# A four-layer post-norm stack on one core: projections and first row maxima in one stage, the first attention's last pair served by VectorE

## The chip, the cores and the metric

The kernel runs on one core of one Trainium2 chip. The metric is the device time of one execution in microseconds. TensorE (PE in the rows) has a weight load of its own (PEld); DVE is VectorE, ACT ScalarE, POOL GpSimd, SP SyncE, which here only issues DMAs.

## The reference

Four layers follow each other on x of 2 x 2048 x 256 float32, each with a residual and a layer norm: softmax attention with a decay, a quantized gated FFN, a linear attention, a mixture of experts. The change lies in the first alone:

```python
N_HEAD = 16                                    # hd = 16
q = (x @ Wq.T + bq).reshape(B, T, H, hd)       # k and v likewise
scores = jnp.einsum('bqhd,bkhd->bhqk', q, k) * scale
decay = jnp.exp(-alpha * jnp.abs(idx[:, None] - idx[None, :]))
attn = jax.nn.softmax(scores * decay, axis=-1)
out = jnp.einsum('bhqk,bkhd->bqhd', attn, v).reshape(B, T, D)
x = _layernorm(x + (out @ Wo.T + bo), axis=-1)
```

## The kernel before

The first attention works on 16 **pairs** of heads (8 for each of the two batches) and is built in four blocks, each closed by a barrier of all engines.

**Clearing.** In `open_sems` GpSimd clears and steps every semaphore, one after the other, while the other engines wait.

**`stage_tables`.** GpSimd writes distances (`toep`, `grow`, `c4`) and the unit matrix `ident`, ScalarE takes exponentials, VectorE splits the inverse decays into three bfloat16 parts, and SyncE stores them in DRAM as `w6`. `toep` holds the decay of every distance, so that any 128x512 piece of the decay matrix is a slice of it.

**`stage_project`.** A hardware loop over 8 chunks of 512 tokens. For each chunk and each half `jt` of the 256 columns TensorE multiplies out q and k into `ps_qk`; ScalarE adds the bias (L245, L248) into `full`; GpSimd makes the copies LEFT and RIGHT of q, scaled by `grow` (L269). Each of the four variants RAW, KEY, LEFT, RIGHT is then split into three bfloat16 parts whose sum is the float32 value: ScalarE casts the high part (L256), VectorE subtracts it (`rest`, L287), casts the middle part (L291) and subtracts again for the low part (L294). SyncE writes `part` to DRAM (`scr`, four DMAs of 384 KB a half; L201). The values v go to `vsb` (L300) and in one DMA a batch to `vscr` (L210). VectorE first clears all of `vsb`.

**`stage_attention`, first block.** GpSimd clears rows of both `p2` buffers (L497), SyncE loads `w6` into them.

**`stage_attention`, second block.** SyncE loads pair 0: `p1` (12 DMAs, L539), `p1` of pair 1 (12), `p2` (12 of L549 and 6 of L539), the values. Before a pair's scores are exponentiated, the maximum of every row is needed: 128 **tiles** a pair, each one matmul of 96x128 by 96x512 (L635) into one of three banks of `ps_r`, and one VectorE operation that multiplies by a slice of `toep` and takes the maximum (L702, with a short read of the accumulator behind it). `fold` reduces the 128 results, `turn` transposes them, and VectorE splits them (L714 to L722); SyncE stores them and loads them back as extra rows of `p2` (L575) and, broadcast, as `mb` (L577). Body `first` of `walk` does 128 tiles of pair 0 and 26 of pair 1 (`SKEW`) with nothing beside them; bodies `lead`, `mid`, `late` interleave the 64 score units of a pair with the tiles of the next; body `last` has units alone.

A **unit** is 512 queries of both heads by 128 keys: two matmuls into one of two halves of `ps_s` (L657), the exponential, and eight value matmuls a unit (L673). 48 of a pair's 64 units are exponentiated by ScalarE right from PSUM (L791). The 16 that straddle the diagonal take another way: ScalarE copies the scores to `tb` (L781), GpSimd multiplies by `toep` (L749) and adds `mb` (L752), ScalarE exponentiates (L788). The order of the units is written out in `SCORE_ORDER` and `EXP_ORDER`; `tb` has four places. After 16 units ScalarE evacuates the sums (L768), TensorE transposes them (L680), VectorE divides (L730, L732).

## Time and profile before

| | us |
|---|---|
| median of 3 runs (3662.7 to 3696.17) | 3683.9 |
| the profiled execution: its time | 3656.15 |
| its span, first to last instruction | 3654.5 |
| first tile of the row maxima | 274.7 |
| first score of pair 0 | 377.7 |
| last evacuation of pair 15 | 1887.8 |

Over the span TensorE is shown busy for 85%, VectorE for 69%, ScalarE for 48% and GpSimd for 40%. Such shares are means over stages that differ: until 377.7 us there is projection and row maxima, until 1888 us the attention of 16 pairs, behind it the other three layers. A matmul's length in the rows is partly modelled, so that TensorE's share reads high.

### The profile page before, as it was taken

Reading aid. Unit: us, or ns where it says so; the run is one execution under the profiler, and the core shown is the slowest. Engines: PE = TensorE matmul, PEld = TensorE weight load, DVE = VectorE, ACT = ScalarE, POOL = GpSimd, SP = SyncE. Lnnn points to the kernel's source line nnn. Section 1 sums busy time; section 2 is a strip of 40 time slices with the busy share of each in tenths; the row PEclk is TensorE's granted clock in tenths of the full one; section 3 lists DMA queues with packets and bytes.
Section 4 is the critical chain, followed back from the end, with each engine's and each line's share of the span. In section 5 each row is a group of like instructions: output and inputs, shape, how many; then the busy total and the mean of one; then the engine's idle time right before and its main releaser. Section 6 shows DMA issues by size and latency. Waiting matters only on the chain. (4 is left out here: it accounts for less than half of the span.)

```text
span 3654.5 us, 67295 instructions
## 1 busy us (share of the span) xinstructions
PE 3093.8 (85%) x22820; PEld 1725.1 (47%) x22821; DVE 2528.3 (69%) x6769; ACT 1738.5 (48%) x2072; POOL 1445.1 (40%) x745
## 2 busy tenths in 40 slices
PE   3619999999999999999953378887999996999997
PEld 1301333333333333333313244444666665999995
DVE  5739999999999999999516767773555554333334
ACT  2300788888888888888861112221222222211112
POOL 2320677877777878777850000000001102111110
PEclk8855999999999999999986689998999997999998
DMA  2852333333443333333013100003000003555555
GB/s 77 225 148 55 83 86 86 87 87 86 87 86 85 84 85 81 84 84 84 31 27 62 34 18 18 11 0 108 13 13 18 20 13 119 186 177 184 179 181 184
DMA packets 197622, 308.68 MB, mean 84 GB/s; under 512 B 86224, under 2 KB 142384, under 8 KB 195184
## 3 DMA queue, kind: packets, MB, share of 16 engines
q1 hardware_dynamic: 188576, 282.09, 29.6%
q0 software_dynamic: 7632, 22.16, 1.7%
q8 instruction: 151, 2.47, 0.3%
q10 hardware_dynamic: 1152, 1.05, 0.1%
q14 instruction: 111, 0.91, 0.1%
HBM read 238.91 MB, written 62.13 MB: 82 GB/s over the span
## 5 line engine op out<-in xcount | busy, mean ns | idle before, releaser
L702 DVE CUSTOM_DVE_ANT_0 ps_r<-ps_r,toep 128x512 f32<-128x512 f32 x2048 | 1353.0, 717 | 129.3 <-PE ps_r L635 89.2
L791 ACT ACTIVATE prob<-ps_s,csc 128x1024 f32<-128x1024 f32 x768 | 831.1, 1120 | 142.3 <-PE ps_s L657 120.6
L635 PE MATMUL ps_r<-p 96*128 96x512 bf16 x2048 | 740.5, 400 | 89.0 <-DMA p<-scr_scratch 74.8
L749 POOL TENSOR_TENSOR tb<-tb,toep 128x1024 f32<-128x1024 f32 x256 | 606.6, 2369 | 407.6 <-ACT tb L781 369.4
L657 PE MATMUL ps_s<-p 120*128 120x512 bf16 (+1 forms) x2048 | 610.7, 380 | 32.7 <-ACT tb L781 25.7
L752 POOL TENSOR_TENSOR tb<-tb,mb 128x1024 f32<-128x1024 f32 x256 | 605.7, 2366 | 20.1
L673 PE MATMUL ps_o<-prob,vp 128*32 128x256 f32 x8192 | 548.2, 385 | 1.9 <-ACT prob L788 1.5
L635 PEld LDWEIGHTS ps_r<-p 96*128 96x128 bf16 x2048 | 197.6, 97 | 562.6 <-DVE mp L702 341.5
L781 ACT ACTIVATE tb<-ps_s 128x1024 f32<-128x1024 f32 x256 | 263.7, 1030 | 174.7 <-PE ps_s L657 173.3
L673 PEld LDWEIGHTS ps_o<-prob,vp 128*32 128x32 f32 x8192 | 213.6, 109 | 270.2 <-issue 177.8
L657 PEld LDWEIGHTS ps_s<-p 120*128 120x128 bf16 (+1 forms) x2048 | 189.3, 98 | 244.6 <-ACT tb L781 63.8
L702 DVE DVE_READ_ACCUMULATOR2_ANT mp<- 128x1 f32 x2048 | 289.4, 141 | 0.0
L2115 ACT ACTIVATE e_aT<-e_u 128x1024 f32<-128x1024 f32 x71 | 75.0, 1057 | 421.2 <-DVE e_u L2186 421.2
L788 ACT ACTIVATE prob<-tb 128x1024 f32<-128x1024 f32 x256 | 272.4, 1064 | 3.2 <-POOL tb L752 3.2
L1475 POOL DMA_INDIRECT slots_scratch<-l_xh,l_place x64 | 62.7, 980 | 527.2 <-DVE l_xh L1800 510.1
L2061 PEld LDWEIGHTS ps_eu<-e_hT,moe_w 128*128 128x128 f32 x2272 | 266.4, 193 | 7.6 <-DVE e_hT L2177 4.0
L2061 PE MATMUL ps_eu<-e_hT,moe_w 128*128 128x128 f32 x2272 | 267.0, 276 | 3.4 <-DVE e_hT L2177 3.4
L2079 PE MATMUL ps_ed<-moe_w,e_aT 128*128 x1136 | 257.0, 379 | 0.8 <-DVE e_y L2232 0.8
L2154 POOL DMA_INDIRECT ytok_scratch<-e_y,e_name x71 | 69.2, 974 | 463.4 <-DVE e_y L2232 463.4
L2186 DVE TENSOR_TENSOR e_u<-ps_eu,moe_cols 128x1024 f32<-128x1024 f32 x71 | 87.0, 1225 | 210.2 <-PE ps_eu L2061 210.2
L2079 PEld LDWEIGHTS ps_ed<-moe_w,e_aT 128*128 128x128 f32 x1136 | 210.3, 190 | 26.9 <-issue 1.2
L1139 PE MATMUL ps_u<-wgu,xs 128*128 128x512 f32 (+1 forms) x384 | 161.5, 571 | 4.6 <-DMA xs<-xqT 4.6
(304 smaller groups left out, 3263.0 us busy)
## 6 DMA issues: line engine op xcount, KB each, us to landing
moe_w<-in_W_dram SPq DMA_DIRECT2D x79, 1024.0 KB, 11.8
p<-scr_scratch SPq DMA_DIRECT2D x288, 192.0 KB
mb<-mrow_scratch SPq DMA_DIRECT2D x16, 2048.0 KB, 8.3
scr_scratch<-part SPq DMA_DIRECT2D x64, 384.0 KB, 6.0
p<-scr_scratch SPq DMA_DIRECT2D x96, 128.0 KB
moe_pt<-slots_scratch SPq DMA_DIRECT2D x72, 132.0 KB, 2.1
vscr_scratch<-vsb SPq DMA_DIRECT2D x2, 4096.0 KB, 15.9
vp<-vscr_scratch SPq DMA_DIRECT2D x16, 512.0 KB, 22.9
```

The lines of the kernel that those rows point to most:

```text
L635: pe.matmul(ps_r[:, bank, :], buf[:, hh, 0, qt * P:(qt + 1) * P], buf[:, hh, 1, kc * CH:(kc + 1) * CH], start=True, stop=True)\
L657: mm = pe.matmul(ps_s[:, n % 2, hh, :], buf[0:rows, hh, KEY, kb * P:(kb + 1) * P], buf[0:rows, hh, var, qb * CH:(qb + 1) * CH], start=True ...
L673: mm = pe.matmul(out.rearrange("p (j c) -> p j c", c=P), vp[whose.par][:, kb, hh, :], prob[:, m % RING, hh, :].rearrange("p (j f c) -> p f ...
L702: dve.tensor_tensor_reduce(ps_r[:, bank, :], ps_r[:, bank, :], toep[:, col:col + CH], 1.0, -3.0e38, ALU.mult, ALU.max, mp[:, whose.par, hh ...
L749: pool.tensor_tensor(tb[:, k % DIAGS], tb[:, k % DIAGS], toep[:, col:col + CH].unsqueeze(1) .broadcast_to([P, 2, CH]), ALU.mult).then_inc( ...
L752: pool.tensor_tensor(tb[:, k % DIAGS], tb[:, k % DIAGS], mb[:, this.par, :, qb * CH:(qb + 1) * CH], ALU.add).then_inc(s["less"], 1)
L781: act.activation(tb[:, k % DIAGS], ps_s[:, (mine - 1) % 2], ACT.Copy).then_inc(s["copied"], 1)
L788: act.activation(prob[:, n % RING], tb[:, k % DIAGS], ACT.Exp).then_inc(s["exp"], 1)
L791: act.activation(prob[:, n % RING], ps_s[:, mine % 2], ACT.Exp, scale=csc[:, qb * TB + kb:qb * TB + kb + 1]).then_inc(s["exp"], 1)
L1139: mm = pe.matmul(ps_u[t % 2][:, lo:hi], xs[:, par, kc, t * P:(t + 1) * P], g["wgu"][:, kc, lo:hi], start=(kc == 0), stop=(kc == KC - 1), s ...
L2061: mm = pe.matmul(ps_u[:, tile.par, f, :], w1[:, tile.par, kc, f * P:(f + 1) * P], hT[:, kc, :], start=(kc == 0), stop=(kc == KC - 1), skip ...
L2079: mm = pe.matmul(ps_d[:, 0:D], aT[:, this.par, f, :], w["w2"][:, bass.ds(e, 1), f, :].rearrange("p a n -> p (a n)"), start=(f == 0), stop= ...
```

## The change

It touches what runs until the first score, and the last pair.

1. **Clearing shared.** Each of the five engines clears a fifth of the semaphores.
2. **One stage in place of three blocks.** `stage_prologue` holds the tables, the projections, the preparation of `p2[0]`, all loads of pair 0, the 128 tiles of pair 0 and the 26 of pair 1, and the store and reload of pair 0's maxima into `p2[0]`. No barrier stands between them. SyncE issues the weight loads ahead of the wait for `w6`.
3. **Sixteen units, written out.** The hardware loop goes. Unit `u` is a batch, a half `jt` and a chunk, in that order, so that after units 0 to 3 all of pair 0's q and k lie in DRAM. TensorE multiplies unit u+1 out in steps 4 and 5 of unit u; values come in the units of `jt` 1. The all-zero LEFT of chunk 0 and RIGHT of chunk 3 are no longer computed (`parts_of`), but still written. `part` has four places in place of two, `full` three.
4. **Split moved.** VectorE keeps the first subtraction (L610, in place in `full`). The middle cast goes to ScalarE (`middle`, L512, one unit later), the last subtraction to GpSimd (`low`, L559).
5. **Tiles inside the units.** From unit 5 on the 128 tiles are spread over 11 x 8 steps (`tiles_behind`), on TensorE and VectorE alike, with two banks. Before the first TensorE waits for `p1` of pair 0. SyncE issues that load behind unit 4, `p2` behind unit 7, `p1` of pair 1 and pair 0's values behind unit 9. The values go to `vscr` in eight DMAs.
6. **`mb` of pair 0** is loaded at the start of the attention block, and GpSimd clears `p2[1]` there.
7. **Last pair.** VectorE multiplies the diagonal units' scores by `toep` right from PSUM (L883) and adds `mb` (L887); GpSimd does nothing, and ScalarE's copy falls away.

```diff
+    flat = [(n, sem) for mine in s.values() for n, sem in mine.items()]
+
+    def clear(eng, share):
+        for n, sem in flat[share::5]:
+            eng.sem_clear(sem)
+            if n not in FROM_ZERO:
+                eng.sem_inc(sem, 1)
...
+GROUPS = 2 * B * QB
+FULLS = 3
+WITH_TILES = 5
+STEPS = 8
+PBANKS = 2
...
+def parts_of(u):
+
+    chunk = u % QB
+    return [KEY] + ([LEFT] if chunk else []) + ([RIGHT] if chunk < QB - 1 else []) + [RAW]
...
+def tiles_behind(u, step):
+
+    many = (GROUPS - WITH_TILES) * STEPS
+    n = (u - WITH_TILES) * STEPS + step
+    return range(TILES * n // many, TILES * (n + 1) // many) if u >= WITH_TILES else range(0)
...
+                for u in range(GROUPS):
+                    b, jt, chunk = place(u)
+                    sp.wait_ge(s["low"], up_to(parts_upto(u + 1)))
+
+                    sp.wait_ge(s[f"out{u % 2}"], up_to(64 * (u // 2)))
+                    for i in range(4):
+                        dst = g["scr"][b * HP + 4 * jt + i, :, :, :, chunk * CH:(chunk + 1) * CH]
+                        sp.dma_start(dst.rearrange("v e d t -> d (v e) t"),
+                                     part[32 * i:32 * i + 32, chunk].rearrange("d v e t -> d (v e) t")).then_inc(s[f"out{u % 2}"], 16)
+                    if jt:
+                        c = chunk_of(u)
+                        sp.wait_ge(s["v_ev"], up_to((c + 1) * TPC))
+                        sp.wait_ge(s["vout"], up_to(16 * c))
+                        cols = TPC * 2 * VW
+                        sp.dma_start(g["vscr"][b * HP:(b + 1) * HP, :, chunk * cols:(chunk + 1) * cols].rearrange("a p n -> p a n"),
+                                     vsb[:, c % 2].rearrange("p a t h d -> p a (t h d)")).then_inc(s["vout"], 16)
+                    if u == QB:
+
+                        sp.wait_ge(s["out1"], up_to(64 * 2))
+                        load_p1(sp, Pair(0, 0))
+                    if u == QB + 3:
+                        load_p2(sp, Pair(0, 0))
+                    if u == QB + 5:
+                        load_p1(sp, Pair(0, 1))
+                    if u == 2 * QB + 1:
+                        sp.wait_ge(s["vout"], up_to(16 * QB))
+                        sp.dma_start(vp[:].rearrange("p t h d -> p (t h d)"), g["vscr"][0]).then_inc(sa["vload0"], 16)
+                sp.wait_ge(sa["setup"], up_to(1))
+                sp.wait_ge(sa["ring_free"], up_to(TILES + TURN + 1))
+                store_maxima(sp, g, sa, mt, mparts)
+                sp.wait_ge(sa["mstore"], up_to(64))
+                load_maxima(sp, g, sa, p2[0], "mload0")
...
+                def tile(slot, j, n):
+                    if slot >= PBANKS:
+                        pe.wait_ge(sa["ring_free"], up_to(slot - PBANKS + 1))
+                    hh, left = divmod(n, TB * QB)
+                    qt, kc = divmod(left, QB)
+                    pe.matmul(ps_r[:, slot % PBANKS, :], p1[j][:, hh, 0, qt * P:(qt + 1) * P],
+                              p1[j][:, hh, 1, kc * CH:(kc + 1) * CH], start=True, stop=True).then_inc(sa["ring_full"], 1)
...
+                    if u == WITH_TILES:
+                        pe.wait_ge(s["cev"], up_to(1))
+                        pe.wait_ge(sa["p1load0"], up_to(192))
+                    for step in range(STEPS):
+                        if step < TPC and u % (2 * QB) >= QB:
+                            values(u, step)
+                        if step in (TPC, TPC + 1) and u + 1 < GROUPS:
+                            project(u + 1, step - TPC)
+                        for n in tiles_behind(u, step):
+                            tile(n, 0, n)
...
+                def middle(u):
+                    chunk = u % QB
+                    for i, var in enumerate(parts_of(u)):
+                        act.wait_ge(s["rest"], up_to(parts_upto(u) + i + 1))
+                        act.activation(part[:, chunk, var, 1, :], full[:, u % FULLS, var, :], ACT.Copy).then_inc(s["mid"], 1)
...
+                def low(u):
+                    for i, var in enumerate(parts_of(u)):
+                        pool.wait_ge(s["mid"], up_to(parts_upto(u) + i + 1))
+                        pool.tensor_tensor(part[:, u % QB, var, 2, :], full[:, u % FULLS, var, :], part[:, u % QB, var, 1, :],
+                                           ALU.subtract).then_inc(s["low"], 1)
...
+                def split(u, i):
+                    var = parts_of(u)[i]
+                    dve.wait_ge(s["hi"], up_to(parts_upto(u) + i + 1))
+                    if var == RAW:
+                        dve.wait_ge(s["scaled"], up_to(scaled_upto(u + 1)))
+                    dve.tensor_tensor(full[:, u % FULLS, var, :], full[:, u % FULLS, var, :], part[:, u % QB, var, 0, :],
+                                      ALU.subtract).then_inc(s["rest"], 1)
...
+                    for step in range(STEPS):
+                        if step < len(parts_of(u)):
+                            split(u, step)
+                        if step >= TPC and u % (2 * QB) >= QB:
+                            values(u, step - TPC)
+                        for n in tiles_behind(u, step):
+                            tile(n, 0, n)
...
+                        elif kind == "score" and not nxt and s_unit(n)[2]:
+
+                            qb, kb, _ = s_unit(n)
+                            k = diag_count(n)
+                            col = OFF + CH * qb - P * kb
+                            dve.wait_ge(s["score"], up_to(this.times(UNITS) + n + 1))
+                            if k == 0:
+
+                                dve.wait_ge(s["exp"], up_to(this.times(UNITS) + EXP0))
+                            dve.wait_ge(s["exp"], up_to(this.times(UNITS) + place_in(SCORE_ORDER, n, EXP_ORDER) - TB + 1 + EXP0))
+                            dve.tensor_tensor(tb[:, k % DIAGS], ps_s[:, n % 2], toep[:, col:col + CH].unsqueeze(1)
+                                              .broadcast_to([P, 2, CH]), ALU.mult).then_inc(s["copied"], 1)
+                            dve.wait_ge(s["copied"], up_to(this.times(TB) + k + 1))
+                            dve.wait_ge(s["mbc"], up_to(this.times(16) + 16))
+                            dve.tensor_tensor(tb[:, k % DIAGS], tb[:, k % DIAGS], mb[:, this.par, :, qb * CH:(qb + 1) * CH],
+                                              ALU.add).then_inc(s["less"], 1)
...
+                        pool.memset(p2[1][ROWS:ROWS + AUG, :, LEFT:RIGHT + 1, :], 0.0).then_inc(s["setup"], 1)
+                        pool.wait_ge(s["setup"], up_to(2))
+                        return
+                    if not nxt:
+                        return
...
-                            if SCORE_ORDER[(mine - 1) % TB] == "d":
+                            if SCORE_ORDER[(mine - 1) % TB] == "d" and nxt:
```

**How the rows move.** On VectorE in one chunk of the projections before (`rest`, `full`, `part` are the variants' buffers; the register rows count semaphores):

```order
L286 REGISTER_ALU
L287 TENSOR_TENSOR rest<-full,part 128x512
L291 CAST part<-rest 128x512 x4
L294 TENSOR_TENSOR part<-rest,part 128x512 x4
L298 ISA
L300 ISA
L300 REGISTER_ALU
L300 TENSOR_TENSOR vsb<-ps_v,bv 128x8x2x16
L298 REGISTER_ALU
L300 ISA
```

and in the change in unit 5, the first with tiles (`ps_pr` are its two banks, `mp` the maxima):

```order
L610 TENSOR_TENSOR full<-full,part 128x512
L626 ISA ps_pr,mp<-ps_pr,toep 128x512
L626 ISA mp 128x1
L626 ISA ps_pr,mp<-ps_pr,toep 128x512
L626 ISA mp 128x1
L610 TENSOR_TENSOR full<-full,part 128x512
L626 ISA ps_pr,mp<-ps_pr,toep 128x512
L626 ISA mp 128x1
L618 TENSOR_TENSOR vsb<-ps_v,bv 128x8x2x16
L626 ISA ps_pr,mp<-ps_pr,toep 128x512
L626 ISA mp 128x1
L618 TENSOR_TENSOR vsb<-ps_v,bv 128x8x2x16
```

The casts and last subtractions are gone from VectorE, and two tile operations stand beside each kind of small operation. On GpSimd, one chunk before:

```order
L264 DMA xc<-in_xT_dram 128x2x512
L267 REGISTER_ALU
L269 TENSOR_TENSOR full<-full,grow 128x512 x2
L267 REGISTER_ALU
L269 TENSOR_TENSOR full<-full,grow 128x512 x2
```

and units 3 to 6 in the change:

```order
L589 MEMSET p_0 24x2x4096
L597 TENSOR_TENSOR full<-full,grow 128x512
L559 TENSOR_TENSOR part<-full,part 128x512 x4
L597 TENSOR_TENSOR full<-full,grow 128x512
L559 TENSOR_TENSOR part<-full,part 128x512 x3
L553 DMA xc<-in_xT_dram 128x2x512
L597 TENSOR_TENSOR full<-full,grow 128x512 x2
L559 TENSOR_TENSOR part<-full,part 128x512 x3
```

Each unit's products now stand ahead of three or four subtractions of the unit before it, and the clearing of `p_0` lies among them. TensorE from unit 1 to unit 5 in the change, where before eight q and k matmuls and eight of v alternated:

```order
L454 MATMUL ps_qk<-xc,w_qkv 128x512 x12
L464 MATMUL ps_v<-w_qkv,xc 128x256 x8
L454 MATMUL ps_qk<-xc,w_qkv 128x512 x4
L464 MATMUL ps_v<-w_qkv,xc 128x256 x2
L474 MATMUL ps_pr<-p_0 128x512
L464 MATMUL ps_v<-w_qkv,xc 128x256 x2
L474 MATMUL ps_pr<-p_0 128x512
L464 MATMUL ps_v<-w_qkv,xc 128x256 x2
L474 MATMUL ps_pr<-p_0 128x512 x2
L464 MATMUL ps_v<-w_qkv,xc 128x256 x2
L474 MATMUL ps_pr<-p_0 128x512
L454 MATMUL ps_qk<-xc,w_qkv 128x512 x2
```

The tiles (`ps_pr<-p_0`) begin in unit 5, each behind the projection matmuls of its step. SyncE's queue in the change around the first load of `p1` (the rows of `p_0` from 48, 32 and 16 partitions):

```order
L415 DMA scr_scratch<-part 32x12x512 x20
L422 DMA vscr_scratch<-vsb 128x8x256
L312 DMA p_0<-scr_scratch 48x1x2048 x2
L312 DMA p_0<-scr_scratch 32x1x2048 x2
L312 DMA p_0<-scr_scratch 16x2048 x2
L312 DMA p_0<-scr_scratch 48x1x2048 x2
L312 DMA p_0<-scr_scratch 32x1x2048 x2
L312 DMA p_0<-scr_scratch 16x2048 x2
L415 DMA scr_scratch<-part 32x12x512 x4
```

Twenty DMAs of `part` (units 0 to 4) and one of `vsb` stand ahead of the first twelve loads, and unit 5's behind them. ScalarE in one quarter of the last pair before (`ot` is the evacuation, `tb<-ps_s` the copy):

```order
L768 ACTIVATE ot<-ps_o 128x256
L781 ACTIVATE tb<-ps_s 128x1024
L791 ACTIVATE prob<-ps_s,csc 128x1024 x2
L788 ACTIVATE prob<-tb 128x1024
L791 ACTIVATE prob<-ps_s,csc 128x1024
L781 ACTIVATE tb<-ps_s 128x1024
L791 ACTIVATE prob<-ps_s,csc 128x1024 x2
L788 ACTIVATE prob<-tb 128x1024
L791 ACTIVATE prob<-ps_s,csc 128x1024
L781 ACTIVATE tb<-ps_s 128x1024
```

and in the change:

```order
L946 ACTIVATE ot<-ps_o 128x256
L969 ACTIVATE prob<-ps_s,csc 128x1024 x2
L966 ACTIVATE prob<-tb 128x1024
L969 ACTIVATE prob<-ps_s,csc 128x1024 x3
L966 ACTIVATE prob<-tb 128x1024
L969 ACTIVATE prob<-ps_s,csc 128x1024 x3
L966 ACTIVATE prob<-tb 128x1024
L969 ACTIVATE prob<-ps_s,csc 128x1024 x2
```

The copies are gone; the exponentials keep their order.

## Rows read from the trace of the kernel before

**Rows 1.** Stretches of the span: start:end, length, busy (count) by engine, clock, DMA.

```profile
0.00:380.00 380.00, 200.11 (x423) 73.17 (x425) 249.92 (x563) 65.91 (x102) 71.50 (x56) 0.70 0.47 128
275.00:375.00 100.00, 92.47 (x154) 15.86 (x152) 99.36 (x307) 0.00 (x0) 0.00 (x0) 0.50 0.27 62
380.00:1800.00 1420.00, 1395.39 (x11590) 536.78 (x11587) 1325.90 (x3990) 1220.55 (x1257) 1135.16 (x480) 1.00 0.37 82
1800.00:1880.00 80.00, 64.76 (x608) 20.69 (x608) 1.99 (x8) 75.21 (x81) 69.93 (x31) 1.00 0.03 4
```

**Rows 2.** Timeline of the first 60 us: start, length, instruction, [idle before].

```profile
17.99 3.43 POOL L97 IOTA toep<- 128x3968 f32 x1 [17.38 <-POOLq L65]
...
33.55 0.39 SPq L193 DMA_DIRECT2D w_qkv<-in_WqT_dram  x1
...
41.20 8.68 PE L226 MATMUL ps_qk<-xc,w_qkv 128*128 128x512 f32 x16 [13.65 <-DMA bv<-in_bv_dram]
...
45.55 2.51 POOL L269 TENSOR_TENSOR full<-full,grow 128x512 f32<-128x512 f32 x2 [9.92 <-ACT full L245]
```

**Rows 3.** Groups by line and shape, 0 to 265 us: busy us, mean ns.

```profile
L269 POOL TENSOR_TENSOR full<-full,grow 128x512 f32<-128x512 f32 x32 | 46.0, 1456 | 110.1 <-ACT full L245 110.1
L287 DVE TENSOR_TENSOR rest<-full,part 128x512 f32<-128x512 f32 x64 | 42.1, 720 | 23.2 <-ACT part L256 21.5 <-DVE vsb L278 0.6
...
L256 ACT ACTIVATE part<-full 128x512 bf16<-128x512 f32 x64 | 35.1, 618 | 50.2 <-DMA scr_scratch<-part 49.6 <-POOL full L269 0.3
L232 PE MATMUL ps_v<-w_qkv,xc 128*128 128x256 f32 x128 | 31.9, 407 | 9.0 <-DVE vsb L300 9.0
...
L497 POOL MEMSET p<- 24x8192 bf16 x2 | 13.8, 6920 | 31.4 <-POOLq L183 31.4
...
L300 DVE TENSOR_TENSOR vsb<-ps_v,bv 128x256 f32 x32 | 11.3, 417 | 3.1 <-DVE part L294 3.1
L248 ACT ACTIVATE full<-ps_qk,bk 128x512 f32<-128x512 f32 x16 | 10.9, 680 | 8.3 <-PE ps_qk L226 8.3
```

**Rows 4.** SyncE's DMA queue in order of time, 0 to 380 us.

```profile
141.22 76.18 SPq L201 DMA_DIRECT2D scr_scratch<-part  x32
218.08 1.03 SPq L210 DMA_DIRECT2D vscr_scratch<-vsb  x1
...
247.61 36.35 SPq L539 DMA_DIRECT2D p<-scr_scratch  x24
284.00 18.05 SPq L549 DMA_DIRECT2D p<-scr_scratch  x12
...
365.26 6.15 SPq L575 DMA_DIRECT2D p<-m_scratch  x8
```

**Rows 5.** Timeline, 190 to 285 us: two casts on VectorE, the first tile.

```profile
199.32 3.57 DVE L291 CAST part<-rest 128x512 bf16<-128x512 f32 x4
...
207.83 1.43 DVE L291 CAST part<-rest 128x512 bf16<-128x512 f32 x4
...
274.70 1.46 PE L635 MATMUL ps_r<-p 96*128 96x512 bf16 x3 [74.76 <-DMA p<-scr_scratch]
```

**Rows 6.** Timeline, 370 to 420 us: the first score and GpSimd's first product.

```profile
377.69 1.06 PE L657 MATMUL ps_s<-p 96*128 96x512 bf16 x2
...
379.96 2.35 POOL L749 TENSOR_TENSOR tb<-tb,toep 128x1024 f32<-128x1024 f32 x1 [132.65 <-ACT tb L781]
```

**Rows 7.** DMA issues on the page: count, KB each, us to landing.

```profile
mb<-mrow_scratch SPq DMA_DIRECT2D x16, 2048.0 KB, 8.3
```

**Rows 8.** Timeline of ScalarE in the last pair: its first and last evacuation.

```profile
1804.94 0.38 ACT L768 ACTIVATE ot<-ps_o 128x256 f32<-128x256 f32 x1 [0.72 <-PE ps_o L673]
...
1887.75 0.38 ACT L768 ACTIVATE ot<-ps_o 128x256 f32<-128x256 f32 x1 [1.19 <-PE ps_o L673]
```

**Rows 9.** Costliest groups on the page: the copy, and VectorE reading PSUM.

```profile
L781 ACT ACTIVATE tb<-ps_s 128x1024 f32<-128x1024 f32 x256 | 263.7, 1030 | 174.7 <-PE ps_s L657 173.3
...
L2186 DVE TENSOR_TENSOR e_u<-ps_eu,moe_cols 128x1024 f32<-128x1024 f32 x71 | 87.0, 1225 | 210.2 <-PE ps_eu L2061 210.2
```

610 lines of the change are left out of this document (321 added, 289 removed).

## The prediction, made before the changed kernel was run

> **What bounds the kernel now.** I read the table of stretches first, then the timeline of each stretch that the change touches. From 380 to 1800 us VectorE is busy for 1325.9 of 1420 us at full clock [rows 1]: the attention goes at VectorE's pace, and the change leaves its order alone there. Behind 1890 us nothing is touched. So only two places can give or lose time: what stands before the first score at 377.7 us [rows 6], and the last pair.
>
> Before the first score the work stands in a row. Clearing holds all engines until 18.0 us; the first projection matmul comes at 41.2, 7.65 us behind the first weight load was issued (33.55) [rows 2]; SyncE stores chunks until 217.4 us and the values from 218.1 [rows 4]; the first tile waits for its load until 274.7 [rows 5]; and 154 tiles run alone, one per 0.65 us (100 us for 154 matmuls), VectorE full, ScalarE and GpSimd at zero, the clock at 0.50, which is the 1.2 GHz level [rows 1]. In all 380 us VectorE is busy for 250 and ScalarE for 66 [rows 1]: there is much to overlap.
>
> **The start, step by step.** *Clearing.* 17.4 us [rows 2] for 157 semaphore instructions is 0.11 us each; a fifth is 31 or 32, 3.5 us, so the engines start at about 4. If the other engines need twice GpSimd's time for one, 7.5; I take 4.
>
> *First matmul.* Three small loads are now issued ahead of the weights, some 1.3 us; with 7.65 us from the weights' issue to the first matmul it falls at 13.
>
> *Units 0 to 4, GpSimd's pace.* GpSimd's first product came 4.35 us behind the first matmul [rows 2], so at 17.4. Up to the last subtraction of unit 4 it has 9 products and 17 subtractions. No row shows a float32 minus bfloat16 subtraction with a bfloat16 result on GpSimd; nearest is the product of the same size, 2.51 us for two, 1.26 each [rows 2], which I take. From below the bound is VectorE's 42.1/64 = 0.66 us [rows 3]; from above there is no row. 26 x 1.26 = 33, the `toep` distances 3.4 [rows 2], the clearing of `p_0` 6.9 [rows 3]: 43, so unit 4 ends at 61. Beside a busy VectorE the product took 1.46 on average [rows 3], 5 us more; I take 63. ScalarE, with two evacuations of 0.68 and seven casts of 0.55 (35.1/64) [rows 3], needs 5.2 us a unit and hides behind that.
>
> *The load of `p1`.* Unit 4's four stores and the first piece of values go ahead, some 6 us, to 69. From the first load of `p1` to the first tile it was 274.7 - 247.6 = 27.1 us [rows 4, 5]. First tile at 96. Bounds: 85, if it was the twelve loads behind them that slowed the first twelve (half of the 36.35 us of issue [rows 4] is 18); 106, if the stores in front hold them up.
>
> *The tile units.* VectorE's work in units 5 to 15: 128 tiles x 0.65 = 83, 39 subtractions x 0.66 = 26, 28 value additions x 0.355 (11.3/32) [rows 3] = 10: 119 us. TensorE's part at full clock is 4.3 us of projection (half of 8.68 [rows 2]) and, in 7 units of 11, 4.0 us of values (16 x 0.25 [rows 3]), beside 12 tiles. It fits, but with two banks VectorE runs dry whenever a projection of about 2 us stands between two tiles: 1.5 us a unit, 15 in all, an estimate from these lengths. 134, so the tiles end at 230. Casts and second subtractions that left VectorE need no cover: ScalarE (5.2) and GpSimd (6.3 to 7.3 a unit) lie well below the 12 us of a unit.
>
> *SyncE's queue* could set a later end. Behind 69 it has 18 us for `p1`, then eleven units of stores, 30 us for `p2` (12 loads in 18.05 [rows 4] and six more at 36.35/24 = 1.5 each give 27; I put 30), 18 for the other `p1`, and seven pieces of values at 3 to 4. A store took 76.18/32 = 2.38 us [rows 4], waits included, so 9.5 a unit; I take 7, since VectorE and not the queue set part of that pace. 69 + 18 + 77 + 30 + 18 + 25 = 237, and unit 15 can't be stored before 232: the queue gets to the maxima's store about 5 us later than VectorE does.
>
> *The end of the stage.* From the 128th tile (275.5 + 128 x 0.65 = 358.7) to the first score (377.7 [rows 6]) it took 19 us: 26 tiles, fold and turn. SyncE's reload of the maxima, 6.15 us [rows 4] and some 5 around it, hides behind the last 22 tiles as before. With 2 us for the change of block and 4 for the queue's lateness the first score falls at 255, **123 us earlier**.
>
> *What the change adds.* `mb` is now issued when the attention starts and lands 8.3 us later [rows 7]; GpSimd's first product started 2.3 us behind the first score [rows 6]. Behind that wait on GpSimd stand all diagonal units, for them ScalarE, and behind its exponentials TensorE's scores with VectorE's tiles. Loss 6 us, between 3 (slack in `tb`'s four places) and 8. GpSimd's clearing of `p_1`, 6.9 us, lies under the same wait.
>
> **The last pair.** Its evacuations at 1804.9 and 1887.75 [rows 8] lie 62 units apart: 1.33 us a unit. ScalarE is busy for 75.2 of 80 us [rows 1], and 16 copies of 1.03 us [rows 9] go. What is left of its 85 us is about 67 of work; TensorE is busy for 64.8 of 80 [rows 1], so it is the next, at nearly the same pace, with two halves of `ps_s` between them. VectorE's 16 products from PSUM cost 1.23 [rows 9] and its 16 additions about 2 x 0.66, 41 us in an engine that was idle (2 of 80 us [rows 1]). 16.5 at best, 5 if TensorE sets the pace; I take **11 us**.
>
> **GpSimd and VectorE side by side.** Two groups of casts on VectorE took 3.57 and 1.43 us, the first while GpSimd multiplied [rows 5], and GpSimd's product 1.46 instead of 1.26. But the same engine's operation of double width took 2.35 beside tiles [rows 6], 1.18 for this width. By the rows, tiles don't slow it; subtractions on VectorE may. The Trainium skill, "GPSIMD Engine Reference", section "Key points", says that GpSimd shares its SBUF interfaces with VectorE and is in contention with instructions in a two-port mode or with two SBUF inputs. By that rule the tiles, with one input in PSUM, are free, as the row shows; the first subtraction is not, and were GpSimd slowed in the whole start as in the projections before, unit 4 would end at 66 and not 61.
>
> **Sum.** 123 - 6 + 11 = 128. The profiled execution took 3656.15 us, which gives 3528. The median of the runs, 3683.9, lies 28 above it, and the runs scatter by 33; I forecast for the median: 3684 - 128 = **3556**. The bounds of the terms (first tile 85 to 106, last pair 5 to 16, `mb` 3 to 8) span 3537 to 3576.
>
> **Rivals.**
> *The queue sets the end (0.15).* At 9.5 us a unit SyncE's sum is 27 higher; the first score falls near 283: 3584. For it: ScalarE waited 49.6 us for stores [rows 3]. Against: `part` has four places now, and all-engine idleness is gone.
> *It overlaps better (0.15).* First tile at 85, no dry banks, stores at 6 us a unit: first score near 228, last pair at its best: 3526.
> *The clock stays at 1.2 GHz (0.06).* It did for 100 us of tiles [rows 1]. Then TensorE needs twice as long: in a unit with values about 7 + 8 + 5 us, without 13; 7 x 20 + 4 x 13 = 192 in place of 134: 3614. Against: a TensorE that is the bound has no gaps, and in these tiles it had one behind each.
> *Slower than before (0.01).* GpSimd's new subtraction is the one unpriced operation, and 56 of them stand in a row with 24 products. Were it slow enough, GpSimd would set the whole stage: 17 + 30 + 12 + 56 x + 20 us to the first score. It loses when that passes 383 (the gain of the last pair less the wait for `mb`), from x = 5.4 us, four times the product. At 6 us it would be 3716.
> *The last pair gives nothing (0.05).* If VectorE's product answers TensorE later than ScalarE's copy did (1.23 against 1.03) and the pace stays: 3567, inside the forecast's own range.
>
> **How the numbers follow.** The forecast keeps 0.58. No change is measured within 1% (37 us), which is about what a measurement of this kernel can tell. All cases but the last slow one, and part of the clock's, lie beyond it: faster 0.97, same 0.02, slower 0.01. The range takes in the queue and the better overlap with some scatter of the runs: 3515 to 3600; it leaves out the clock, the slow case and the tails.
>
> **What would show it.** In the profile after: engines start near 4 us, first projection matmul near 13; GpSimd's subtraction near 1.26 us; first tile between 85 and 106, with VectorE and TensorE idle before it; tiles of pair 0 done near 230, clock above 0.5; first score near 255; a gap of GpSimd of some 9 us at the start of the attention; about 1.15 us a unit in the last pair, no row of ScalarE writing `tb`. The forecast is wrong if the first tile waits much beyond 106, if ScalarE waits for stores in each unit, or if the attention of pairs 0 to 14 changes its pace, for which I see no reason.

## The result, and the profile after

| | before | after |
|---|---|---|
| median, us (four runs each) | 3680.2 (3662.7 to 3696.2) | 3554.6 (3550.9 to 3556.6) |
| the profiled execution: time | 3656.15 | 3555.51 |
| its span | 3654.5 | 3553.5 |
| first tile of the row maxima | 274.7 | 104.9 |
| last tile of pair 0 read | 358.7 | 259.7 |
| first score of pair 0 | 377.7 | 281.7 |
| last evacuation of pair 15 | 1887.8 | 1784.4 |

The kernel before has one run more here than in the forecast (then 3683.9). The ratio is 0.966, 95% interval 0.961 to 0.970. The median fell by 125.6 us and the forecast of 3556 was 1.4 us off. But the two profiled executions lie only 100.6 apart, where the sum of the forecast said 128. So the total came out right with terms that did not; the sections below take the two apart. "Last tile of pair 0 read" is the end of VectorE's 128th tile operation.

**Stretches.** Columns as in [rows 1]; the first two stretches end at VectorE's first tile and at the last tile of pair 0, the third at the end of the stage.

```profile
0.00:105.50 105.50, 29.46 (x73) 14.54 (x75) 35.58 (x38) 37.07 (x55) 52.41 (x44) 0.74 0.48 136
105.50:260.00 154.50, 116.42 (x317) 53.39 (x316) 122.06 (x324) 52.58 (x94) 68.49 (x57) 0.83 0.74 185
260.00:280.00 20.00, 15.33 (x26) 2.59 (x25) 19.44 (x57) 0.00 (x0) 0.00 (x0) 0.50 0.55 155
280.00:1700.00 1420.00, 1394.69 (x11557) 536.63 (x11557) 1328.08 (x3998) 1215.11 (x1254) 1136.89 (x479) 1.00 0.37 82
1700.00:1780.00 80.00, 70.38 (x674) 23.47 (x678) 41.09 (x40) 69.66 (x72) 4.89 (x3) 1.00 0.09 31
```

The attention between is as it was: VectorE 1328 of 1420 us, against 1326 in [rows 1]. Nearly all the difference lies ahead of 282 us and in the last pair. In the tile units VectorE is busy for 122 of 154.5 us, with 32 us empty; ahead of them it is empty for 70 of 105.

**The start.** SyncE's queue in order of time (start, length of the issues, instruction, count), which answers to [rows 2, 4]:

```profile
5.99 0.41 SPq L394 DMA_DIRECT2D alpha<-in_alpha_dram  x1
...
39.32 33.56 SPq L415 DMA_DIRECT2D scr_scratch<-part  x20
72.99 1.46 SPq L422 DMA_DIRECT2D vscr_scratch<-vsb  x1
74.51 14.92 SPq L312 DMA_DIRECT2D p<-scr_scratch  x12
...
151.96 9.30 SPq L322 DMA_DIRECT2D p<-scr_scratch  x12
161.31 6.75 SPq L312 DMA_DIRECT2D p<-scr_scratch  x6
168.16 23.78 SPq L415 DMA_DIRECT2D scr_scratch<-part  x8
191.98 16.16 SPq L312 DMA_DIRECT2D p<-scr_scratch  x12
...
256.24 7.62 SPq L415 DMA_DIRECT2D scr_scratch<-part  x4
263.96 1.27 SPq L422 DMA_DIRECT2D vscr_scratch<-vsb  x1
265.33 4.98 SPq L346 DMA_DIRECT2D m_scratch<-mparts  x3
...
273.04 6.17 SPq L356 DMA_DIRECT2D p<-m_scratch  x8
280.42 0.36 SPq L741 DMA_DIRECT2D mb<-mrow_scratch  x1
```

The engines start at 6 (forecast 4, before 17.9). The twenty stores of units 0 to 4 stand in one block of 33.6 us without a gap, 1.7 us each. The load of `p1` is issued at 74.5 (forecast 69), and its consumer begins 30.4 us later (27.1 before):

```profile
104.86 0.63 PE L474 MATMUL ps_pr<-p 96*128 96x512 bf16 x1
...
105.53 0.70 DVE L626 CUSTOM_DVE_ANT_0 ps_pr<-ps_pr,toep 128x512 f32<-128x512 f32 x1 [38.54 <-PE ps_pr L474]
```

Groups by line and shape, 0 to 280 us (busy, mean ns, idle before and who ended it), which answer to [rows 3]:

```profile
L626 DVE CUSTOM_DVE_ANT_0 ps_pr<-ps_pr,toep 128x512 f32<-128x512 f32 x154 | 104.0, 704 | 62.7 <-PE ps_pr L474 62.1
L559 POOL TENSOR_TENSOR part<-full,part 128x512 bf16<-128x512 f32 x56 | 69.9, 1275 | 13.8 <-ACT part L512 13.4
...
L610 DVE TENSOR_TENSOR full<-full,part 128x512 f32<-128x512 f32 x56 | 57.4, 1039 | 21.0 <-ACT part L545 20.8 <-DVE vsb L661 0.2
...
```

GpSimd's subtraction, which no row of before priced, takes 1.275 us: the value taken. VectorE's takes 1.04 on average and not 0.66 (0.84 on average for the 38 from 105 us on, 1.47 for the 18 before). VectorE's waits by cause, 60 to 280 us (total, times, longest):

```profile
DVE ps_pr L626 <- PE ps_pr L474: 62.1, 24, 38.5
DVE vsb L618 <- DMA vscr_scratch<-vsb: 6.2, 1, 6.2
DVE full L610 <- ACT part L545: 2.4, 2, 2.0
```

38.5 is the wait for the first tile. The other 23.6 + 6.2 + 2.4 = 32.2, with 122.1 of work, make up the 154.3 us of the tile units.

The waits for tiles aren't spread evenly. Between 145 and 204 us lie the waits of units 8 to 11, the ones with tiles and without values: 14.9 us, 3.7 a unit. In the seven other units it is 8.7 us, 1.2 a unit. Stretches of the tile units:

```profile
108.00:145.00 37.00, 28.82 (x97) 14.11 (x95) 33.27 (x91) 15.02 (x27) 20.57 (x18) 1.00 0.63 180
145.00:204.00 59.00, 42.74 (x92) 15.66 (x92) 43.63 (x111) 20.02 (x36) 25.87 (x21) 0.74 0.78 163
```

and the two projection pieces of one of the four units (four matmuls each), with the waits behind them:

```profile
162.71 3.41 PE L454 MATMUL ps_qk<-xc,w_qkv 128*128 128x512 f32 x4
166.18 1.88 PE L454 MATMUL ps_qk<-xc,w_qkv 128*128 128x512 f32 x4
166.37 0.70 DVE L626 CUSTOM_DVE_ANT_0 ps_pr<-ps_pr,toep 128x512 f32<-128x512 f32 x1 [2.26 <-PE ps_pr L474]
168.31 0.70 DVE L626 CUSTOM_DVE_ANT_0 ps_pr<-ps_pr,toep 128x512 f32<-128x512 f32 x1 [1.18 <-PE ps_pr L474]
```

The first piece takes 3.41 us at a granted clock of 0.55 (162.0 to 166.2 us), the second 1.88 at 1.00. The first pieces of all four units take 3.2 to 3.6 us, and the waits behind them are 2.9, 2.3, 2.0 and 3.1 us; in the other units each piece takes 1.88, and no wait behind one is above 0.9. Ahead of each slow piece TensorE had done tiles alone, mostly single matmuls of 0.4 to 0.6 us with a gap before each.

**The start of the attention** answers to [rows 6]:

```profile
280.41 6.92 POOL L916 MEMSET p<- 24x8192 bf16 x1 [26.06 <-POOLq L391]
287.41 2.36 POOL L927 TENSOR_TENSOR tb<-tb,toep 128x1024 f32<-128x1024 f32 x1
...
281.69 1.06 PE L823 MATMUL ps_s<-p 96*128 96x512 bf16 x2
```

**The last pair** answers to [rows 8, 9]: ScalarE's evacuations, and VectorE's two operations between 1700 and 1785 us:

```profile
1710.00 0.38 ACT L946 ACTIVATE ot<-ps_o 128x256 f32<-128x256 f32 x1 [0.29 <-PE ps_o L839]
1729.00 0.38 ACT L946 ACTIVATE ot<-ps_o 128x256 f32<-128x256 f32 x1 [0.29 <-PE ps_o L839]
...
1784.41 0.38 ACT L946 ACTIVATE ot<-ps_o 128x256 f32<-128x256 f32 x1 [1.19 <-PE ps_o L839]
```

```profile
L887 DVE TENSOR_TENSOR tb<-tb,mb 128x1024 f32<-128x1024 f32 x16 | 19.6, 1225 | 0.6
L883 DVE TENSOR_TENSOR tb<-ps_s,toep 128x1024 f32<-128x1024 f32 x16 | 19.6, 1224 | 32.9 <-PE ps_s L823 24.2 <-ACT prob L966 8.7
```

The evacuations lie 74.4 us apart in all; before it was 82.8 [rows 8].

**The sum by the two traces.** First score 96.0 earlier; from there to the first evacuation of the last pair 1428.3 against 1427.2 (1804.94 - 377.69), 1.1 lost; last pair 8.4 gained: 103.3. The rest of the span takes 1769.1 against 1766.8, which leaves 101.0.

### The profile page after: what moved, and what is told of

Same layout as the page of the kernel before. It is cut to its first block and busy times, and to the rows that moved or that the text cites. A ratio compares the mean times of both kernels' runs of the same rounds, so it can differ in the third digit from the quotient of the medians.

```text
span 3553.5 us, 66603 instructions
## 1 busy us (share of the span) xinstructions
PE 3058.9 (86%) x22820; PEld 1725.4 (49%) x22821; DVE 2496.0 (70%) x6665; ACT 1748.3 (49%) x2104; POOL 1425.7 (40%) x760
## 5 line engine op out<-in xcount | busy, mean ns | idle before, releaser
L870 DVE CUSTOM_DVE_ANT_0 ps_r<-ps_r,toep 128x512 f32<-128x512 f32 x1894 | 1252.3, 716 | 69.9 <-PE ps_r L799 30.5
L927 POOL TENSOR_TENSOR tb<-tb,toep 128x1024 f32<-128x1024 f32 x240 | 568.0, 2367 | 264.0 <-ACT tb L959 238.0
L799 PE MATMUL ps_r<-p 96*128 96x512 bf16 x1894 | 646.8, 383 | 8.3 <-DVE mp L870 4.3
L930 POOL TENSOR_TENSOR tb<-tb,mb 128x1024 f32<-128x1024 f32 x240 | 567.8, 2366 | 18.8
L799 PEld LDWEIGHTS ps_r<-p 96*128 96x128 bf16 x1894 | 181.5, 96 | 403.9 <-DVE mp L870 257.3
L870 DVE DVE_READ_ACCUMULATOR2_ANT mp<- 128x1 f32 x1894 | 266.2, 141 | 0.0
L959 ACT ACTIVATE tb<-ps_s 128x1024 f32<-128x1024 f32 x240 | 247.0, 1029 | 31.1 <-PE ps_s L823 29.7
## 6 DMA issues: line engine op xcount, KB each, us to landing
moe_w<-in_W_dram SPq DMA_DIRECT2D x79, 1024.0 KB, 11.8
```

The source lines that it names most:

```text
L799: pe.matmul(ps_r[:, bank, :], buf[:, hh, 0, qt * P:(qt + 1) * P], buf[:, hh, 1, kc * CH:(kc + 1) * CH], start=True, stop=True)\
L870: dve.tensor_tensor_reduce(ps_r[:, bank, :], ps_r[:, bank, :], toep[:, col:col + CH], 1.0, -3.0e38, ALU.mult, ALU.max, mp[:, whose.par, hh ...
L927: pool.tensor_tensor(tb[:, k % DIAGS], tb[:, k % DIAGS], toep[:, col:col + CH].unsqueeze(1) .broadcast_to([P, 2, CH]), ALU.mult).then_inc( ...
L930: pool.tensor_tensor(tb[:, k % DIAGS], tb[:, k % DIAGS], mb[:, this.par, :, qb * CH:(qb + 1) * CH], ALU.add).then_inc(s["less"], 1)
L959: act.activation(tb[:, k % DIAGS], ps_s[:, (mine - 1) % 2], ACT.Copy).then_inc(s["copied"], 1)
```

## The experiments

Eleven kernels ran, three of them unedited. "Marks" below are times in the trace: first tile, first score, last evacuation. The unedited changed kernel ran twice more beside the others. The first time:

> The changed kernel once more, unedited, as the standard for the runs beside it. Both theories expect 3551 to 3557 us, first tile at 104.9 us, first score at 281.7 us, last evacuation at 1784 us.

3554.72 (3547.61 to 3555.27), marks 104.6, 281.5, 1786.1. The second time (below) the marks were 106.0, 283.6, 1792.3. These repetitions say what a single trace can tell: unedited, the first tile moves by 1.4 us and the first score by 2.1; from the first score to the first evacuation of the last pair it takes 1428.3, 1430.2 and 1434.2 us; and behind the last evacuation the eleven traces of the changed kernel and its variants take from 1758 to 1774 us. Differences below these are not read as effects of an edit.

### Clearing by GpSimd alone

```diff
-        for n, sem in flat[share::5]:
+        for n, sem in (flat if share == 0 else []):
```

> The changed kernel, but GpSimd clears all semaphores again. Theory: nothing else runs at that time and everything behind it shifts, so +11 to +12 us (the engines start near 17.5 us in place of 6.0), about 3566. Rival: the start is set by the landing of the weight loads and by the wait for the pair's first load, and part of the shift is absorbed there: +0 to +5 us.

3571.3 (3567.5 to 3579.1); marks 116.6, 293.1, 1797.9: each 11.6 to 12 later. SyncE's first DMA moved from 5.99 to 17.76. The shared clearing is worth 11.7 us at every mark, to the 2 us that a trace can tell, and nothing behind it absorbs that. The medians lie 16.6 apart. The other 5 us must come from behind the last evacuation, where the edit changes nothing and where three unedited traces took from 1759.5 to 1769.1 us.

### The last pair by GpSimd again

```diff
-                        elif kind == "score" and not nxt and s_unit(n)[2]:
+                        elif kind == "score" and False:
...
-                    if not nxt:
-                        return
...
-                            if SCORE_ORDER[(mine - 1) % TB] == "d" and nxt:
+                            if SCORE_ORDER[(mine - 1) % TB] == "d":
```

> The changed kernel, but the last pair's diagonal units go by ScalarE's copy and GpSimd again. Theory: ScalarE set that pair's pace, so its evacuations lie 82.8 us apart again in place of 74.4, +8.4 us, about 3563. Rival: the shorter last pair comes from what the start left behind (buffers, the clock) and not from the copies: +0 to +3 us.

The evacuations in ScalarE's timeline:

```profile
1714.03 0.38 ACT L944 ACTIVATE ot<-ps_o 128x256 f32<-128x256 f32 x1 [0.72 <-PE ps_o L839]
...
1796.52 0.38 ACT L944 ACTIVATE ot<-ps_o 128x256 f32<-128x256 f32 x1 [1.19 <-PE ps_o L839]
```

They lie 82.5 us apart, against 74.4 in all ten other traces of the changed kernel: VectorE's service of the last pair is worth 8.1 us. (The first score came at 284.7 here, though nothing ahead of it was edited: scatter of the start.) The times were 3556.8, 3560.4, 3581.8 and 3585.6, in two groups, which the trace's 8 us do not explain; the first two have a granted clock of 0.935 and 0.933, the last two 0.923.

### Each tile multiplied twice

The idea was that half of VectorE's dry spells came from TensorE's clock, and that more matmuls would raise it. The second matmul writes the same tile again; it stands in steps with no other matmul and in the 26 tiles at the end.

```diff
+                    for again in range(2 if twice else 1):
+                        mm = pe.matmul(ps_r[:, slot % PBANKS, :], p1[j][:, hh, 0, qt * P:(qt + 1) * P],
...
+                    mm.then_inc(sa["ring_full"], 1)
```

> The changed kernel, where TensorE does the matmul of a tile twice (same operands, same bank, same result) in the steps with no other matmuls: in the units without values all but the two projection steps, in the others the last two steps, and all 26 tiles of pair 1 behind the units. Nothing is left out. Theory: VectorE's 23.6 us of waiting for tiles between 105 and 260 us come half from TensorE at 1.2 GHz (mean clock 0.83 there, 0.50 behind 260): with more work the clock stays up, the waits fall to 12 to 16 us and the first score comes 5 to 10 us earlier. Rival: the waits come from two banks alone, whatever the clock: no change or a loss of 1 to 5 us.

3564.3 (3556.7 to 3567.8), marks 106.1, 287.9, 1792.9: slower by 10 us, with the first score 6.4 later, nearly all of it in the doubled tail. Stretches as above:

```profile
105.50:260.00 154.50, 125.48 (x375) 52.95 (x375) 123.32 (x321) 52.59 (x94) 68.50 (x57) 0.88 0.73 186
260.00:286.00 26.00, 24.73 (x53) 3.48 (x51) 21.23 (x59) 0.00 (x0) 0.00 (x0) 0.50 0.42 117
```

The granted clock of the tile units rose from 0.83 to 0.88, and VectorE waited for tiles in them until 260 us for 61.8 - 39.1 = 22.7 us (62.0 - 38.5 = 23.5 in the unedited one beside it): hardly less. In the tail TensorE is shown busy for 95% and the clock stayed at the 1.2 GHz level. The forecast of this run failed: doubling tiles brought neither the waits down nor the first score forward. That doesn't clear the clock, though. From 145 to 204 us the waits were 14.9 us again, and the first pieces of those four units again ran slow, 3.0 to 3.6 us at a granted clock of 0.50 to 0.64. The edit raised the mean clock, and not the clock of the pieces behind which VectorE waits. No run here raised that one.

### The projection pieces halved

TensorE does unit u+1's projection in two pieces of four matmuls (1.9 us each at full clock, up to 3.6 at the 1.2 GHz level) in steps 4 and 5. Here they are four of two matmuls, in steps 2 to 5.

```diff
-                        if step in (TPC, TPC + 1) and u + 1 < GROUPS:
-                            project(u + 1, step - TPC)
+                        if 2 <= step < 6 and u + 1 < GROUPS:
+                            project(u + 1, (step - 2) // 2, (step % 2,))
```

> The changed kernel, but the next unit's projection is cut into four halves of about 1 us in steps 2 to 5, with tiles between them, in place of two pieces of 1.9 us in steps 4 and 5. Same matmuls. Theory: VectorE runs dry behind a piece that is longer than two banks cover; its waits for tiles fall from 23.6 to 8 to 14 us and the first score comes 8 to 14 us earlier. Rival: the waits only move, since TensorE has the same work in a unit: 0 to 3 us.

3544.8 (3540.9 to 3552.4), ratio to before 0.965 (0.960 to 0.971); marks 105.1, 272.5, 1779.9. VectorE's waits in it:

```profile
DVE ps_pr L627 <- PE ps_pr L475: 50.9, 22, 39.1
```

The waits for tiles beside the first fell from 23.6 to 11.8 us, half, as the length of the pieces did. Two banks hold two tiles, some 1.4 us of VectorE's work, and a piece of 1.9 us outlasts that; so does the half piece where the clock is low (two matmuls in 1.9 us, against 1.0 at full clock). In the units of the low clock (142 to 200 us here) the waits are 6.2 us where they were 14.9, in the others 5.6 where they were 8.7. The length of a piece is thus shown as a cause, at either clock. The unedited changed kernel didn't run beside this one; against its three traces the first score is 9 to 11 us earlier.

### VectorE makes the low parts of units 0 to 4

If GpSimd's pace set the first tile, taking 17 subtractions from it should bring the tile forward by ten us or more. (`HEAD` is 5; GpSimd's clearing of `p_0` no longer waits for the subtractions before it, either.)

```diff
-                    if u:
+                    if u > HEAD:
                         low(u - 1)
...
+                    if 0 < u <= HEAD:
+                        for i, var in enumerate(parts_of(u - 1)):
+                            dve.wait_ge(s["mid"], up_to(parts_upto(u - 1) + i + 1))
+                            dve.tensor_tensor(part[:, (u - 1) % QB, var, 2, :], full[:, (u - 1) % FULLS, var, :],
+                                              part[:, (u - 1) % QB, var, 1, :], ALU.subtract).then_inc(s["low"], 1)
```

> The changed kernel, but VectorE does the last subtraction of units 0 to 4 (17 operations), where it stands idle; GpSimd begins with unit 5. Theory: GpSimd's row of operations sets the time of unit 4's parts (66.4 us) and with them the first load of p1; 17 x 1.3 us less in that row bring the first tile from 104.9 to 90 to 96 us and the whole by 8 to 14 us, about 3544. The first subtraction on VectorE (1.47 us a piece there) should fall to about 0.9, since GpSimd holds it up less. Rival: the stores to DRAM (20 DMAs in 33.6 us of queue) or ScalarE set that time: 0 to 4 us.

3557.2 (3553.8 to 3560.0); marks 101.9, 278.8, 1783.9: 3 us at the first tile, and no gain in the time. The parts of unit 4 are ready near 57 us instead of 66.4, but SyncE's queue reads

```profile
37.60 33.34 SPq L416 DMA_DIRECT2D scr_scratch<-part  x20
71.06 1.38 SPq L423 DMA_DIRECT2D vscr_scratch<-vsb  x1
```

the same block of 33 us from 37.6 on. The 1.7 us by which it starts earlier are most of the 3. The stores, not GpSimd, set the first load of `p1`: the rival was right.

### Both of these

> The edits of the two kernels before together: last subtractions of units 0 to 4 on VectorE, projections in four halves. Theory: they lie in different stretches and add, about 3534. Rival: SyncE's queue, which ended 4 us behind VectorE's units, becomes the bound for the maxima's store: no more than 5 to 8 us in all.

3544.7 (3537.0 to 3550.8); marks 102.3, 271.1, 1777.7. The two gains didn't add: the time is that of the halves alone (3544.8), where the theory said 3534. The first tile is 2.8 us earlier than with the halves alone, the first score 1.4. The store of the maxima was issued at 255.6, right behind unit 15's values (253.5, 2.0 us): in this version the end of the stage waits for SyncE's queue as much as for the tiles.

### The stores begin earlier

On top of both, SyncE's eight DMAs of `w6` and their waits move behind unit 5, since until 37 us they hold up stores whose data is ready at 28.9.

```diff
-                sp.wait_ge(s["cev"], up_to(1))
-                for r, e in enumerate(K_PARTS):
...
+                    if u == QB + 1:
+                        sp.wait_ge(s["cev"], up_to(1))
+                        for r, e in enumerate(K_PARTS):
```

> The version with VectorE's subtractions in the head and the projection pieces in halves, and SyncE's eight DMAs of w6 with their two waits moved behind unit 5's stores. In the trace of the version without this last move the last subtraction of unit 0 ended at 28.87 us, while SyncE stood at its wait for wt and w6 until 37.4, and its twenty stores then took 32.9 us without a gap. Theory (the queue of stores sets the first tile): the stores begin near 29, are done near 62 to 64, the first load of p1 is issued near 64 to 66, the first tile comes near 95 (102.3 there), and the first score 7 us earlier, near 264; the time falls from 3545 to about 3538. Rival (the end of the stage waits for SyncE's later queue, not for the tiles): the first tile comes 7 us earlier all the same, but the first score by 3 us or less, and the time stays within 3 of 3545. A second rival (units 0 to 4 themselves set it): the stores of unit 4 wait for its parts until 57 and end near 66, so that first tile comes near 97.

3538.5 (3537.9 to 3542.8), ratio to before 0.965 (0.959 to 0.971); marks 96.4, 267.6, 1770.9. SyncE's queue:

```profile
28.95 36.61 SPq L409 DMA_DIRECT2D scr_scratch<-part  x20
65.66 1.59 SPq L416 DMA_DIRECT2D vscr_scratch<-vsb  x1
67.30 13.64 SPq L313 DMA_DIRECT2D p<-scr_scratch  x12
```

The stores start 8.5 us earlier and take 3.7 more, so the second rival has part of it; the first tile comes 5.9 earlier and the first score 3.5. (The last evacuation is 6.7 earlier, but 3 of that lie in the attention, within its scatter.) This is the fastest version: 14 us below the changed kernel that ran beside it (3552.9). The gain over the version before it, 6 us in the time, compares two kernels that didn't run side by side.

### The scatter of the kernel before

The forecast took 28 us from the profiled execution to the median as scatter. The kernel before ran unedited five rounds:

> The kernel before, unedited. Its profiled execution took 3656.15 us, its other runs 3662.7 to 3696.2, while the changed kernel's lie within 6 us of each other and at its profiled time. Theory: the kernel before has a varying stretch that the change took away; several runs will again spread over 20 to 35 us, and if the profiled one is a longer one its trace shows the stretch. Rival: the spread came from the chip at that time: the runs now lie within 6 us.

Its 12 times and the 41 of the same kernel that ran beside the experiments fall in **two groups** with nothing between: 22 from 3647.0 to 3664.5 us, at a granted clock of 0.917 to 0.922 over the span, and 31 from 3676.5 to 3700.9, at 0.904 to 0.910. Their medians are 3654.9 and 3685.9, 31 apart. The execution profiled first (3656.15) was one of the first group; this run's (3685.21) one of the other. The last evacuation is at 1887.4 and 1887.8, and from 1900 to 2500 us the clock is 0.81 in both. The stretches behind it, first of the execution of 3685.21 us, then of the one of 3656.15:

```profile
2500.00:2800.00 300.00, 276.97 (x2687) 190.30 (x2686) 152.67 (x422) 74.78 (x136) 23.45 (x24) 0.88 0.05 18
2800.00:3200.00 400.00, 349.82 (x3120) 268.73 (x3117) 196.95 (x594) 99.84 (x181) 51.89 (x53) 0.85 0.20 66
```

```profile
2500.00:2800.00 300.00, 275.73 (x2844) 189.33 (x2845) 162.40 (x450) 78.02 (x143) 23.46 (x24) 0.95 0.07 24
2800.00:3200.00 400.00, 348.88 (x3182) 275.42 (x3179) 199.99 (x593) 103.00 (x183) 55.76 (x57) 0.93 0.24 79
```

This is the linear attention, which no edit touches. The same 1024 matmuls of its line 1577 take 348 ns in the one and 304 in the other; the first matmul of the experts' line 2061 comes at

```profile
3107.74 5.57 PE L2061 MATMUL ps_eu<-e_hT,moe_w 128*128 128x128 f32 x32 [1.37 <-DVE e_hT L2177]
```

against 3078.68, 29.1 us apart, and behind it, from 3200 to 3650 us, the clock is 0.98 and 0.99. So of the recorded theory the first half held, several runs again far apart; that the change took a varying stretch away is the next question.

### Does the change remove the lower group, or was it chance?

> The changed kernel without an edit, five rounds, for more samples. Kernel before fell into two groups some 29 us apart (3647 to 3665 at a granted clock of 0.917 to 0.921, 3676 to 3696 at 0.904 to 0.910), of which a trace of either shows that they differ in the linear attention layer alone, which the change doesn't touch. Theory A (the phase at which that layer is reached decides, and the change has moved it to one where the clock is nearly always high): all runs lie in 3547 to 3557. Theory B (chance of the execution or the chip, the same for both kernels: some half to two thirds of the runs in the slow group): of ten runs at least two lie near 3580, and the ratio to before comes to 0.971.

3552.9 (3547.4 to 3560.8), six runs, clock 0.931 to 0.934. With the first result and the first repetition that is 14 runs of the changed kernel, **none in a lower group**. At the share that the kernel before had (31 of 53) 14 such runs would come by chance with 0.42 to the 14th, about 5 in a million. Taken against the 24 runs of the kernel before that stood beside ten of the 14 (15 of 24 in the lower group), the ten would come by chance once in some 20,000. Chance of the execution is no explanation, if executions are independent of each other.

```diff
-            clear(pool, 0)
+            for again in range(28):
+                clear(pool, 0)
```

> The changed kernel, in which GpSimd clears and steps its fifth of the semaphores 28 times instead of once, so that everything starts some 96 to 100 us later, as late as the kernel before reached its first score; nothing else is changed. Theory A (phase: the clock granted in the linear attention layer depends on how long after the start, or after the first matmuls, it is reached): a group of runs some 25 to 30 us above the other appears, 3650 and 3680, as in the kernel before. Theory B (what ran before that layer decides, not when): one group alone, near 3652. Theory C (chance): the same share of slow runs as the unedited changed kernel has in this call.

3642.8 (3629.5 to 3664.1), first score at 371.7 and last evacuation at 1874.9: 88 and 83 us later than in the unedited kernel beside it, still 6 and 13 us ahead of the kernel before. Nine runs lie from 3629.5 to 3648.3 at 0.932 to 0.937, three from 3661.2 to 3664.1 at 0.924 to 0.926, their medians 22.6 apart. So a lower group seems to come back by starting later, but for a quarter of the runs and not for more than half; none of the three theories is confirmed as written, and against none of 14 the three of 12 could still be chance. The restored last pair had two of four such runs (clock 0.923), though it starts no later (first score 284.7); clearing by GpSimd alone, which does start later (11.7 us), had none (0.928 to 0.931). That points at the last pair itself: with it served by VectorE and without the delay, none of 38 runs (the 14 and 24 of six variants) was in a lower group. But the four runs with GpSimd's last pair are few, and the three delayed ones had VectorE's. What decides between the groups **stays open**: the moment at which the linear attention is reached is at most part of it.

## Why the prediction was right or wrong

**Where it acts: right.** Between the first score and the last pair the two first traces differ by 1.1 us, and behind it by 2.3, both less than repetitions differ. That the attention goes at VectorE's pace, from which the prediction argues, no run tested: TensorE is shown busy for 1395 of those 1420 us.

**Clearing: right in kind, 2 us short.** 6.0 and not 4; worth 11.7 by its own experiment. The first projection matmul came at 15.6, forecast 13, mostly from the same 2 us.

**Units 0 to 4: a near number, the wrong cause.** "GpSimd's pace" gave 63 for unit 4's parts; it was 66.4, with 1.275 us for the unpriced subtraction. But SyncE's queue was then still busy with stores until 72.9, and without GpSimd's part of the work it was busy until 70.9. The step that failed is "Unit 4's four stores and the first piece of values go ahead, some 6 us": I priced only the last unit's stores on a queue that was behind by more than that. Twenty at 1.68 us from 39.3 are 33.6. I had the row for it (2.38 us a store, [rows 4]) and used it for the queue's end alone, not for its start. SyncE's wait for `w6`, which the forecast didn't price, held the stores up; moving it behind them brought their start 8.5 us forward, their end 4.8 and the first tile 5.9.

**The load of `p1`: 30.4 against 27.1.** Together the first tile came at 104.9, inside 85 to 106 at its upper end, "if the stores in front hold them up". 8.9 us of the sum's error.

**The tile units: the largest miss, 154 and not 134.** VectorE's work was 122 (forecast 119). The term "1.5 us a unit, 15 in all" of dry spells measured 23.6. Its mechanism was right, as the halved pieces show, and at full clock its price was not too low: 1.2 us a unit in seven units. What the term had wrong is the clock under which it was worked out: "TensorE's part at full clock". In four units the first piece ran near the 1.2 GHz level, and the waits were 3.7 us a unit. Had the four waits behind these pieces (10.3 us) been as long as those behind the second pieces of the same units at full or nearly full clock (0.75 to 1.5), some 6 us would be gone; this is an estimate from the trace, for no run raised the clock there. Two waits were not in the sum, 6.2 us once for the store of values that stood behind the loads of `p2` on SyncE's queue, and 2.4 for ScalarE's casts. With 3 us more work they make the 20 us.

**The end of the stage: 22.0 us, forecast 25.** SyncE's queue was late as said (unit 15's values at 264.0, the 128th tile at 259.7), 4.3 us and not 5.

**`mb`: 6 forecast, not settled.** From the first score to the last pair the three unedited traces took 1.3, 3.2 and 7.2 us longer than the mean of before's two (1427.0). "Loss 6 us, between 3 and 8" is neither confirmed nor refuted by that, and no run isolated it. GpSimd had its first product right behind its clearing of `p_1`, at 287.4, 5.7 us behind the first score where it had been 2.3; `mb` had landed at 287.2. ScalarE waited 1.8 us at its first diagonal exponential: the rest of the delay went into the slack of `tb`.

**The last pair: 11 forecast, 8.4 measured, 8.1 by its experiment.** 16 copies went, and a quarter of 16 units now takes 19.0 us. In the stretch to 1780 TensorE is busy for 70.4 of 80 us and ScalarE for 69.7: neither is full, with two halves of `ps_s` between them; which of the two sets the pace is not shown. VectorE's product and addition were priced at 1.23 and 1.32, and took 1.22 each.

**Sum.** 8.9 (first tile) + 20.2 (units) - 3.0 (end) + 0.6 between TensorE's and VectorE's first tile = 26.7 us, by which the first score (281.7) missed 255; +2.6 from the last pair and -4.9 from the attention give the 103 of the traces in place of 128, and 2 more were lost behind. By the two first traces the gain is 101, less than the bounds of the terms allowed. (They allow 110, not 108: 3556 + 10 + 6 + 2 is 3574, where the prediction has 3576.)

**The step that made it come out right** is "the median lies 28 above it, and the runs scatter by 33; I forecast for the median". That took the 28 us as something the changed kernel keeps. They come from the share of executions in the lower clock group, which the changed kernel has not shown in 14 runs. Against the group of before at the higher clock (3654.9) the changed kernel's median is 100.3 lower, just what the traces say; the other 25 us come from the clock in a layer that the change doesn't touch. Two errors of like size and other sign met: the median was hit by luck. Had the changed kernel kept both groups in the same shares, its median would have been near 3585 (3685.9 - 101), inside the range.

**Rivals.** *The queue sets the end* was part of the truth at the other end, the start. *It overlaps better* failed in all three of its points. *The clock stays at 1.2 GHz* failed for the stage as a whole, 0.83 in the units; but it was right for parts of four of them (0.50 to 0.57 at their first pieces), and most of the dry spells' excess stands there, and in the last 26 tiles it was 0.50. *Slower* had its condition, a subtraction above 5.4 us, and it took 1.275. *The last pair gives nothing* was 8.1 us off.

## What to carry to other kernels

When a stage is made to overlap, sum each DMA queue from its first entry, waits included, and not only behind the last producer: here an early wait for a small table and twenty stores of 1.7 us set the moment of the first tile, and moving the wait behind them brought it 5.9 us forward. A piece of work on TensorE that is longer than what its consumer has in hand empties the consumer each time; cutting it to that length helps at either clock. Read the granted clock where the consumer waits, and not as the mean of a stage: here 0.83 hid pieces at half speed, with 15 of 24 us of the waits in the four units that had them, and an experiment that raised the mean missed them. Before a profiled time is set against a median, see how the runs group by their granted clock, and in which layer the two groups differ: a shift of 25 us can come from there.
